# Linear attention in a decoder kernel: two buffers for masked state and transposed queries, normalisation on ACT, statistics a tile ahead

## The reference

```
x = x + _L0_attn_ref(_layernorm(x), Wq, Wk, Wv, Wo, norm_const)

def _layernorm(x, axis=-1, eps=1e-05):
    return (x - mean(x)) / sqrt(var(x) + eps)

def _L0_attn_ref(x, Wq, Wk, Wv, Wo, norm_const):      # 16 heads of 8 columns
    q = _l2norm(proj(Wq))          # t / max(norm(t), 1e-12), per head
    k = _l2norm(proj(Wk))
    v = proj(Wv) / C ** sigmoid(norm_const)
    kv = einsum('nhcd,nhce->nhde', k, v)
    attn = einsum('nhcd,nhde->nhce', q, kv)
    return attn.transpose(0, 2, 1, 3).reshape(N, C, d) @ Wo.T
```

## Time and profile before

| | us |
|---|---|
| median of 3 runs | 1929.0 (1927.7 to 1929.32) |
| the profiled execution, its own time | 1931.23 |
| its span, first to last instruction | 1929.4 |
| mean granted clock of TensorE | 0.959 of full |
| the linear attention within the span | from 9.3 to 232.5 |

### The profile page before, as it was taken

How to read it: one execution, slowest core, us unless ns; L and a number is a source line. 1 busy time by engine, 2 the same in 40 slices (tenths; PEclk the granted TensorE clock), 3 DMA queues, 4 the chain that set the end, 5 groups by cost and what they waited for, 6 DMA issues and landing times. The chain is left out here.

```text
span 1929.4 us, 52384 instructions
## 1 busy us (share of the span) xinstructions
PE 1719.7 (89%) x13531; PEld 1481.4 (77%) x13531; DVE 1387.2 (72%) x4413; ACT 1273.6 (66%) x3518; POOL 855.6 (44%) x2194
## 2 busy tenths in 40 slices
PE   5777779999997999996999999799999999289997
PEld 3444458888886999995888888578888888288887
DVE  5777658778885888885888888578888888334443
ACT  4444368888885777775888888478888888122222
POOL 2222145555551222223555555256778777423333
PEclk9999869999998999997999999899999999699999
DMA  8950000000000000000000000000111111099996
GB/s 240 399 222 0 0 12 13 14 12 12 12 12 3 1 0 0 0 1 1 1 0 0 0 0 0 8 23 24 32 34 31 33 32 30 30 279 289 290 281 204
DMA packets 122074, 124.14 MB, mean 64 GB/s; under 512 B 35317, under 2 KB 100488, under 8 KB 122000
## 3 DMA queue, kind: packets, MB, share of 16 engines
q1 hardware_dynamic: 117392, 114.40, 18.8%
q0 software_dynamic: 4320, 8.53, 1.3%
q10 hardware_dynamic: 288, 0.34, 0.1%
HBM read 79.57 MB, written 44.12 MB: 64 GB/s over the span
## 5 line engine op out<-in xcount | busy, mean ns | idle before, releaser
L1036 PE MATMUL xa_ps_o<-xa_vb,xa_pt 128*128 128x96 f32 x2048 | 246.7, 274 | 0.0
L1036 PEld LDWEIGHTS xa_ps_o<-xa_vb,xa_pt 128*128 128x128 f32 x2048 | 239.5, 192 | 0.1
L881 ACT ACTIVATE xa_pt<-xa_ps_pt 128x512 f32<-128x512 f32 x256 | 139.1, 595 | 97.1 <-PE xa_ps_pt L955 97.1
L1203 PE MATMUL ffn_ps_h<-ffn_xdt,w1t 128*128 128x128 f32 x1536 | 184.6, 276 | 0.4 <-ACT ffn_xdt L1169 0.4
L693 DVE TENSOR_REDUCE xa_mx<-xa_ps_s 128x8 f32<-128x512 f32 x256 | 164.9, 686 | 24.8 <-PE xa_ps_s L971 21.2
L1203 PEld LDWEIGHTS ffn_ps_h<-ffn_xdt,w1t 128*128 128x128 f32 x1536 | 179.0, 194 | 0.7 <-ACT ffn_xdt L1169 0.7
L845 POOL TENSOR_TENSOR xa_km<-xa_kt,const_sb 128x256 f32<-128x256 f32 x256 | 152.5, 617 | 37.9 <-ACT xa_kt L894 28.6
L699 DVE TENSOR_TENSOR xa_pr<-xa_ps_s,xa_mx 128x512 f32<-128x512 f32 x256 | 163.6, 679 | 0.2
L971 PE MATMUL xa_ps_s<-xa_km,xa_qm 64*128 64x256 f32 x1024 | 149.9, 412 | 4.0 <-POOL xa_km L845 4.0
L875 ACT ACTIVATE xa_pr<-xa_pr 128x512 f32<-128x512 f32 x256 | 147.2, 622 | 3.6 <-DVE xa_pr L699 0.8
L955 PEld LDWEIGHTS xa_ps_pt<-const_sb,xa_pr 128*128 128x128 f32 x1024 | 111.0, 142 | 41.7 <-issue 41.7
(11 more groups left out here) (271 smaller groups left out, 4776.7 us busy)
## 6 DMA issues: line engine op xcount, KB each, us to landing
exp_w1b<-in_L_ffn_w_dram SPq DMA_DIRECT2D x71, 512.0 KB, 3.7
x_sorted<-no_row SPq DMA_DIRECT2D x1, 34320.0 KB, 91.2
exp_w2b<-in_L_ffn_w_dram SPq DMA_DIRECT2D x71, 256.0 KB, 4.1
xa_cn<-in_ctx_dram SPq DMA_DIRECT2D x128, 64.0 KB, 1.8
exp_xg<-x_sorted SPq DMA_DIRECT2D x71, 66.0 KB, 3.0
xa_mi<-in_mask_BxSxS_ik_dram SPq DMA_DIRECT2D x128, 32.0 KB, 2.1
out_dram<-exp_y,exp_token POOLq DMA_INDIRECT x71
x_sorted<-x_sb,place POOLq DMA_INDIRECT x64, 2.4
```

Source lines behind the costliest of these rows:

```text
L881: nc.scalar.activation(pt[:, 512 * hf:512 * hf + 512], ps_pt[hf][:, :], ACT.Copy).then_inc(s["pt_sb"], 1)
L1036: last = nc.tensor.matmul(ps_o[:, 2 * VW * g:2 * VW * g + av_w], pt[:, P * g:P * g + P], vb[(r + 1) % RING][:, 2 * VW * g:2 * VW * g + av_ ...
L1203: last = nc.tensor.matmul(ps_h[c][:, 0:P], k.w1t[:, j, c, :], xdt[:, :, j:j + S], start=j == 0, stop=j == 2)
```

## The change

Four things, all in `linear_attention`:

- kvm and qt get two buffers each; their writers wait for the attention matmul of tile t instead of t + 1, and PE's L556 reads buffer 1 - q.
- xn is computed by ACT, as Identity with r as scale and shift as bias, as the first instruction of ACT's turn. POOL makes shift with two further instructions. The wait on xt_done stands before it as it stood before L391.
- the floor of the length goes into the scaling: the reciprocal is taken of the length itself, and the scaling takes the smaller of it and 1/1e-12 as it multiplies. L484 and its semaphore go.
- the statistics are made for tile t + 7 rather than t + 6, and all engines run turns from -7. DVE's order becomes: statistics (t + 7), reciprocal (t + 3), mean and variance (t + 7), scaling (t + 3), masked state (t + 2), x (t), sums (t + 4).

The diff:

```diff
--- before.py
+++ after.py
@@ -416,15 +410,16 @@
             return ctx.enter_context(nc.psum_tensor("lin_ps_" + name, [P, w], F32))
         ln = layernorm_memory(nc, k, ctx, "lin")
         xn, xt = sb("xn", [P, D]), sb("xt", [P, P])
-        sq, ss, length = sb("sq", [P, 256]), sb("sum_sq", [P, 32]), sb("length", [P, 32])
-        floored, inv = sb("floored", [P, 32]), sb("inv_length", [P, 32])
+        shift, minus = sb("ln_shift", [P, 1]), sb("ln_minus", [P, 2])
+        sq, ss, length, inv = sb("sq", [P, 256]), sb("sum_sq", [P, 32]), sb("length", [P, 32]), sb("inv_length", [P, 32])
         qk = [sb(f"qk{i}", [P, 256]) for i in range(2)]
         v = [sb(f"v{i}", [P, 2, D]) for i in range(2)]
-        qt = sb("qt", [P, 3, S])
-        kvm, at = sb("kvm", [P, 2, D]), sb("at", [P, P])
+        qt = [sb(f"qt{i}", [P, 3, S]) for i in range(2)]
+        kvm = [sb(f"kvm{i}", [P, 2, D]) for i in range(2)]
+        at = sb("at", [P, P])
         ps_qkv = [ps("qkv0"), ps("qkv1")]
         ps_xt, ps_kv, ps_qt, ps_at, ps_y = (ps(n) for n in ("xt", "kv", "qt", "at", "y"))
-        names = ["consts", "xt_done", "xt_sb", "qkv_done", "sq", "ss", "length", "floored", "inv", "qk", "v_sb",
+        names = ["consts", "product", "shift", "xt_done", "xt_sb", "qkv_done", "sq", "ss", "length", "inv", "qk", "v_sb",
                  "kv_done", "kvm", "qt_sb", "at_done", "at_sb", "y_done", "x_done"]
         s = {n: k.sem("lin_" + n) for n in names}
         nt = k.nt
@@ -440,52 +435,50 @@
 
             @block.vector
             def _(dve):
+                nc.vector.memset(ln["eps"][:, :], LN_EPS)
+                nc.vector.memset(ln["half"][:, :], -0.5)
+                nc.vector.memset(minus[:, 0:1], -1.0)
                 for q in range(2):
                     nc.vector.memset(v[q][:, :, :], 0.0)
-                nc.vector.memset(qt[:, :, :], 0.0)
-                nc.vector.memset(ln["eps"][:, :], LN_EPS)
-                nc.vector.memset(ln["half"][:, :], -0.5).then_inc(s["consts"], 1)
-
+                    last = nc.vector.memset(qt[q][:, :, :], 0.0)
+                last.then_inc(s["consts"], 1)
                 dve.wait_ge(k.x_in, 16)
 
                 def body(t, q):
                     if isinstance(t, int) and t == 0:
                         dve.wait_ge(k.x_rest, 16)
-                    if live(t + 6):
-                        layernorm_stats(nc, dve, k, t + 6, ln)
-                        dve.wait_ge(ln["stats"], t + 7)
+                    if live(t + 7):
+                        wait(dve, s["shift"], t + 7)
+                        layernorm_stats(nc, dve, k, t + 7, ln)
+                        dve.wait_ge(ln["stats"], t + 8)
+                    if live(t + 3):
+                        dve.wait_ge(s["length"], t + 4)
+                        wait(dve, s["qk"], t + 3)
+                        nc.vector.reciprocal(inv[:, :], length[:, :]).then_inc(s["inv"], 1)
+                    if live(t + 7):
+                        layernorm_var(nc, ln)
                     if live(t + 3):
                         dve.wait_ge(s["inv"], t + 4)
                         wait(dve, s["kv_done"], t + 2)
-                        nc.vector.tensor_tensor(qk[1 - q][:, :].rearrange("p (g d) -> p g d", d=HD),
-                                                ps_qkv[1 - q][:, 0:256].rearrange("p (g d) -> p g d", d=HD),
-                                                inv[:, :].unsqueeze(2).broadcast_to([P, 32, HD]), ALU.mult).then_inc(s["qk"], 1)
-                    if live(t + 6):
-                        layernorm_var(nc, ln)
+                        nc.vector.scalar_tensor_tensor(qk[1 - q][:, :].rearrange("p (g d) -> p g d", d=HD),
+                                                       inv[:, :].unsqueeze(2).broadcast_to([P, 32, HD]), 1.0 / L2_EPS,
+                                                       ps_qkv[1 - q][:, 0:256].rearrange("p (g d) -> p g d", d=HD),
+                                                       ALU.min, ALU.mult).then_inc(s["qk"], 1)
                     if live(t + 2):
                         dve.wait_ge(s["kv_done"], t + 3)
-                        wait(dve, s["at_done"], t + 2)
-                        nc.vector.tensor_tensor(kvm[:, :, :], ps_kv[:, 0:2 * D].rearrange("p (b c) -> p b c", b=2),
+                        wait(dve, s["at_done"], t + 1)
+                        nc.vector.tensor_tensor(kvm[q][:, :, :], ps_kv[:, 0:2 * D].rearrange("p (b c) -> p b c", b=2),
                                                 k.blk[:, :].unsqueeze(1).broadcast_to([P, 2, P]), ALU.mult).then_inc(s["kvm"], 1)
+                    if live(t):
+                        dve.wait_ge(s["y_done"], t + 1)
+                        xs = k.x[:, col(t), :].rearrange("p a d -> p (a d)")
+                        nc.vector.tensor_tensor(xs, xs, ps_y[:, 0:D], ALU.add).then_inc(s["x_done"], 1)
                     if live(t + 4):
                         dve.wait_ge(s["sq"], t + 5)
                         wait(dve, s["length"], t + 4)
                         nc.vector.tensor_reduce(ss[:, :], sq[:, :].rearrange("p (g d) -> p g d", d=HD), axis=AX.X,
                                                 op=ALU.add).then_inc(s["ss"], 1)
-                    if live(t + 6):
-                        wait(dve, s["xt_done"], t + 6)
-                        layernorm_scale(nc, dve, k, t + 6, ln, xn[:, :]).then_inc(ln["normed"], 1)
-                    if live(t):
-                        dve.wait_ge(s["y_done"], t + 1)
-                        xs = k.x[:, col(t), :].rearrange("p a d -> p (a d)")
-                        nc.vector.tensor_tensor(xs, xs, ps_y[:, 0:D], ALU.add).then_inc(s["x_done"], 1)
-                    if live(t + 4):
-                        dve.wait_ge(s["length"], t + 5)
-                        nc.vector.tensor_scalar(floored[:, :], length[:, :], L2_EPS, None, ALU.max).then_inc(s["floored"], 1)
-                        dve.wait_ge(s["floored"], t + 5)
-                        wait(dve, s["qk"], t + 4)
-                        nc.vector.reciprocal(inv[:, :], floored[:, :]).then_inc(s["inv"], 1)
-                pipeline_pairs(dve, nt, 6, body)
+                pipeline_pairs(dve, nt, 7, body)
                 dve.wait_ge(s["x_done"], nt)
 
             @block.gpsimd
@@ -493,19 +486,28 @@
                 pool.wait_ge(s["consts"], 1)
 
                 def body(t):
-                    if live(t + 6):
-                        layernorm_rstd(nc, pool, t + 6, ln)
-                pipeline(pool, nt, 6, body)
+                    if live(t + 7):
+                        layernorm_rstd(nc, pool, t + 7, ln)
+                        pool.wait_ge(ln["rstd"], t + 8)
+                        nc.gpsimd.tensor_tensor(minus[:, 1:2], ln["mv"][:, 0:1], ln["r"][:, :], ALU.mult).then_inc(s["product"], 1)
+                        pool.wait_ge(s["product"], t + 8)
+                        nc.gpsimd.tensor_tensor(shift[:, :], minus[:, 0:1], minus[:, 1:2], ALU.mult).then_inc(s["shift"], 1)
+                pipeline(pool, nt, 7, body)
 
             @block.scalar
             def _(act):
                 act.wait_ge(s["consts"], 1)
 
                 def body(t, q):
+                    if live(t + 6):
+                        act.wait_ge(s["shift"], t + 7)
+                        wait(act, s["xt_done"], t + 6)
+                        nc.scalar.activation(xn[:, :], k.x[:, col(t + 6), :].rearrange("p a d -> p (a d)"), ACT.Identity,
+                                             bias=shift[:, 0:1], scale=ln["r"][:, 0:1]).then_inc(ln["normed"], 1)
                     if live(t + 2):
                         act.wait_ge(s["kv_done"], t + 3)
-                        wait(act, s["at_done"], t + 2)
-                        nc.scalar.activation(qt[:, 0:3:2, :], ps_qt[:, 0:P].rearrange("p (b c) -> p b c", b=2),
+                        wait(act, s["at_done"], t + 1)
+                        nc.scalar.activation(qt[q][:, 0:3:2, :], ps_qt[:, 0:P].rearrange("p (b c) -> p b c", b=2),
                                              ACT.Copy).then_inc(s["qt_sb"], 1)
                     if live(t + 4):
                         act.wait_ge(s["qkv_done"], t + 5)
@@ -521,13 +523,13 @@
                         nc.scalar.activation(at[:, :], ps_at[:, 0:P], ACT.Copy).then_inc(s["at_sb"], 1)
                     if live(t + 4):
                         act.wait_ge(s["ss"], t + 5)
-                        wait(act, s["floored"], t + 4)
+                        wait(act, s["inv"], t + 4)
                         nc.scalar.activation(length[:, :], ss[:, :], ACT.Sqrt).then_inc(s["length"], 1)
                     if live(t + 5):
                         act.wait_ge(s["xt_done"], t + 6)
                         wait(act, s["qkv_done"], t + 5)
                         nc.scalar.activation(xt[:, :], ps_xt[:, 0:P], ACT.Copy).then_inc(s["xt_sb"], 1)
-                pipeline_pairs(act, nt, 6, body)
+                pipeline_pairs(act, nt, 7, body)
 
             @block.tensor
```

(5 more changed lines are left out.)

## The result

| | before | after |
|---|---|---|
| median of the runs beside each other, us | 1928.35 (1927.53 to 1929.32, 4 runs) | 1966.45 (1963.83 to 1967.0, 4 runs) |
| after to before | | 1.0196, 95% interval 1.0183 to 1.0209 |
| profiled execution, us; its span | 1931.23; 1929.4 | 1963.83; 1962.0 |
| end of the linear attention in the span | 232.51 | 267.35 |
| mean turn, from one masked state to the next, us | 3.30 | 3.87 |

The change costs 38 us between the medians and 32.6 between the profiled executions. The end of the linear attention moves by 34.8 us, and no later stage gains or loses more than 1.5: the cross attention of layer 0 starts 34.5 later, the experts 33.5.

What follows compares the result with a forecast made beforehand. ACT and PE working in turn bound the linear attention, 3.31 us a tile. With 3.79, 60 turns times 0.48 = 28.8, plus 2.7 + 2.7 - 2, gave +32.2 us: median 1961, range 1944 to 1975.

Steps and rivals of the forecast that it cites:

- The wait that moves: In the linear attention, xn first on ACT waits for L562, PE's last instruction of the turn, 0.11 us after L556.
- xn's cost: xn on ACT lengthens each linear attention turn by 0.37 us from start to start, bounds 0.17 and 0.48.
- The handover: From the end of PE's turn to the start of ACT's in the linear attention: 0.09 us.
- PE's part: PE's stretch of the linear attention turn grows by 0.11, from 1.58 to 1.69 us, starting 0.05 after ACT's L529.
- DVE and POOL hidden: DVE's savings and POOL's two more instructions stay off the path of the 3.79 us linear attention turn.
- Start and end: In the linear attention, pipeline filling adds 2.7 us, a later full clock 2.7, and the last turns give 2 back.
- the sum: Linear attention turns plus the stage's start and end: +32.2 us, giving a span of 1961.6 us.
- Rival B: TensorE's clock drops for the whole linear attention: some 80 us more, 2040 us; chance 0.04.
- Rival C: Identity and Sqrt share no table, so each linear attention turn has two loads: 164 us, 2093; chance 0.02.
- Rival D: xn's wait is met before the attention matmul ends, so ACT works under PE's turn: 49 us less, 1880; chance 0.06.

## Why the prediction was right

*The wait that moves.* Right. Indices and timeline gave xn the place behind the last matmul of PE's turn, and the waits show it there; undoing the buffers left the turn at 3.87, and moving the transpose changed the sign.

*xn's cost.* Right in kind, a little small: 0.37 forecast, 0.40 measured, 0.492 us for the instruction. The estimate of 0.386 from start to start (the Trainium skill, ScalarE: Activation LUTs, section "What ACT_TABLE_LOAD costs") is nearer than my row of the self attention.

*The handover.* This term was mis-sized. I took the 0.09 of the queries' copy, which reads a fixed address; xn reads a tile of x whose address ACT works out, and the handover is 0.18. The fixed address gave back 6.7 us, 0.08 x 60 = 4.9 of it in the turns. With both, the turn grew by 0.58 (3.31 to 3.89) rather than 0.48, 6 us more over 60 turns.

*PE's part.* Right: 1.69, and 0.05 after xt.

*DVE and POOL hidden.* Right for after: the shift is ready at 183.73, xn needs it at 185.69. But "a tile of lead covers it" holds only for xn in first place. In the middle the chain closes over two turns (3.27 a turn), at the end over one (4.40).

*Start and end.* The forecast was +2.7, +2.7 and -2. Measured, the clock came up at 30.2 us instead of 21.0, after four slow projections instead of two, as supposed; the projection of tile 1 starts at 20.60 instead of 17.20. The first masked state came 4.4 us later (25.6 instead of 21.2), the 59 turns from there to the 60th took 33.7 more (3.87 instead of 3.30 each), and the last turns gave 3.3 back. So of the stage's 34.8 start and end are 1.1, where I had 3.4 for them. The profiled span, 1962.0 against the 1961.6 of the sum, agrees more closely than its terms: the turns cost 5 more, start and end 2 less, the later stages 2 less. That the sum came within 0.4 us is luck to that extent. The median is 5.4 above the 1961 named: 0.4 of that is the span, the rest the step from one execution to the median, which I took as 2.2 below the profiled one, as in before, and which was 2.6 above it here (1966.45 against 1963.83). One profiled execution does not fix that step.

*The clock.* Rival B did not come: from 30.2 to 269.2 us the granted clock stayed full at a busy share of 64%. It was nearer than its chance of 0.04 says: xn twice, a turn 0.4 longer, was enough for the two levels to alternate, and so was xn last. My grounds for 0.04 were weak. The stretch that I set against the rival, 602 to 610 us at the full clock, stands right ahead of a fall: the clock went to 1.2 GHz at 611.5, after PE had been busy for 0.82 us of the last 2 of that stretch and for none of the time from 610 on. Two stretches do not show from which point the clock decides, and no run here does.

*Table loads.* Rival C is dead: Identity and Sqrt alternate in each turn, and the stage has one load, and by that the trace agrees with the Trainium skill (ScalarE: Activation LUTs, section "Table sets: the hidden batching unit"):

```profile
L527 ACT ACT_TABLE_LOAD x1 | 1.3, 1283 | 0.0
```

*Rival D.* Its deciding point was the right one, and its 1880 stands against 1892 measured. It supposed PE to be the bound at 2.5; the turn is 2.65, with xn waiting for the transpose and the statistics for POOL in each. Which loop sets the last 0.15 was not told apart.

The two fastest kernels, 1876.89 and 1875.88, beat before by 51 to 55 us and after by about 90, both with xn on DVE. Of the change's four parts, then, the two buffers gain, the floor within the scaling makes no difference to the whole time (4.4 us within the stage), and the loss comes with the normalisation on ACT as placed. The runs that move xn within ACT's turn (1928 and 1996) or its transpose within PE's (1892) show it: the same instructions gain or lose by their place. The statistics a tile ahead were not tried without xn on ACT.

## What to carry to other kernels

Before a step moves to another engine, count which instruction frees its buffer and where that one stands in its engine's turn: a single-buffered producer behind the last matmul of a turn puts two engines in series, and second buffers elsewhere gained nothing here. Two engines can both be idle for much of the time (PE a third, ACT half) and still set the pace, so the load taken off a third one (30 us of DVE here) is no gain. Write down each loop over one turn and over two, with every engine in it, before you place a step: the position of one instruction was worth 74 us on PE, and on ACT between 1928 and 1996.

## What the hardware showed beside

xn with an address made at run time starts 0.09 us later behind its wait than with a fixed one (0.18 against 0.09). The register step of 0.05 us that belongs to it runs behind the wait, though it needs nothing that the wait brings.

TensorE's clock was at 2.4 GHz through turns of 3.89 us, and went back and forth between 2.4 and 1.2 GHz through turns that take 4.27 and 4.40 at the full clock. With xn last, where PE is not in the loop that sets the pace, this cost nothing that the turns show. With xn twice it did: 0.4 us a turn on ACT cost 76 us (1966.45 to 2042.89), of which 24 are the 60 times 0.4 itself.

Where the loop over four turns comes round, one turn is 0.45 us longer in the kernel with two buffers alone (3.26 against 2.81), and 0.64 and 0.44 in the two fastest ones (3.06 and 2.86 against 2.42), where the turn behind it is some 0.2 shorter. In before and after the mean shows nothing of it.
